# First attention of an eight-layer kernel: value products of two key tiles in a row, twice per unit

## The chip, the cores and the metric

One core of a Trainium2 chip runs the whole program. A core has five engines that are tied together by semaphores only: TensorE (matrix products, which read the working memory SBUF and write the accumulators, PSUM), VectorE, ScalarE, GpSimd and SyncE (which here issues the transfers, DMAs). The metric is the device time of one execution in microseconds (us). Smaller is better.

## What is computed

A residual stream `x` of 8 sequences x 512 tokens x 128 channels goes through four attention-like layers and four mixtures of experts. The change touches the first layer alone, an attention with 16 heads of 8 channels and a relative bias:

```python
xn = layernorm(layernorm(x)) * ln_g + ln_b
q, k, v = split_heads(xn @ w_qkv + b_qkv)          # 16 heads of 8
scores = einsum('bhqd,bhkd->bhqk', q, k) * scale
attn = softmax(scores + relative_bias(w_rel), axis=-1)
out = einsum('bhqk,bhkd->bhqd', attn, v)
x = x + merge_heads(out) @ w_out + b_out
```

## The kernel before

`relative_attention` (from line 839) is the stage. Its work is cut into 32 units: for each of the B = 8 sequences b, NG = 4 groups g of GH = 4 heads; unit u = 4 b + g. All engines walk through the units in an order that is written out by hand, each in its own function in the block, and wait for one another by semaphores.

For softmax the maximum over the keys is needed first. So the scores are made twice. `max_score(u, s)` (line 1099) makes a product of 128 queries by 512 keys in bf16 parts, 16 per unit, into one of three PSUM buffers `aps`; VectorE takes its maximum over the keys (`maximum`, line 1329). `turn_maxima` (line 1105) transposes the 16 columns of maxima into the next `aps` buffer, ScalarE copies them (`take_maxima`, line 1256), GpSimd splits them into three bf16 parts, and DMAs put those into rows of `Q`. Two units later `key_scores(u, t)` (line 1111) makes the product of 128 keys by 512 queries with the maximum already subtracted, 16 per unit, two per call, into one of three buffers `sps`, and ScalarE takes the exponential of it into `prob` (line 1293). Here A stands for a product of `max_score` and S for one of `key_scores`.

`values(u, k)` (line 1120) is the product of the probabilities with the values, in fp32: for key tile k (4 of them) four heads, each in its own 32 columns of TensorE, accumulated in the PSUM buffer `ops` over the four k. A fp32 product leaves two records in the trace, so that one call has 8. When all four k are done, ScalarE copies `ops` to `OT` (`copy_outputs`, line 1261). `turn_outputs` (line 1129) transposes it in four pieces into `mps`, and VectorE divides by the sum of the probabilities (`outputs`, lines 1337 and 1339).

Once per sequence there are further pieces of work on TensorE, in fp32, which share the one buffer `mps`: `turn_sequence` and `project` (lines 1136 and 1143) for the sequence before, in units g = 2 and g = 3; `v_part` (1161), `turn_tokens` (1150), `qk_part` (1155) for sequences to come, in units g = 0, g = 1 and g = 2, 3. `project` is followed by `add_output` on VectorE (1346) and by statistics (1350, 1354) in unit g = 3. ScalarE copies what the pieces made after the unit's exponentials, and `copy_sequence` after the fourth exponential of g = 2.

The order on TensorE in unit u: for t_ = 0 to 7 there is A(2 t_), S(2 t_), S(2 t_ + 1), A(2 t_ + 1), where the A belong to unit u + 2 and the S to unit u. After t_ = 0 comes the sequence or the projection, after t_ = 2 the output transposes of unit u - 2, after t_ = 6 the piece for a later sequence, and after t_ = 1, 3, 5, 7 the value products of unit u - 1 with k = 0, 1, 2, 3. At the end stands the turn of the maxima. An A waits until the maximum three buffers back is taken, an S until the exponential three back is done.

On VectorE the maxima s = 0 to 15 come in order, and `outputs(u - 2)` after s = 6. On SyncE each unit has the transfer of the maxima (`store_max`), in two of four units a store of the q or k parts that GpSimd has split (`store_parts`), and the nine loads of a unit three ahead (`load`). The first A of a unit waits for those loads.

Seven further stages follow, each in its own block.

Of the kernel before, what the change touches and what calls it, by code (L numbers as in the profile page):

```python
# [838 lines left out]
def relative_attention(nc, net, d):  # L839
# [16 lines left out]
    with ExitStack() as ctx:  # L856
# [223 lines left out]
        def _(pe):  # L1080
            def claim(*use):
                kind, n = before[use]
                emptied = dict(xt=xt_done, q=pj_done[0], k=pj_done[1], v=pj_done[2], outputs=o_done,
                               sequence=otn_done, project=y_added)[kind]
                pe.wait_ge(emptied, n + 1)

            def max_score(u, s):
                n = SLOTS * u + s
                if n >= 3:
                    v, r = (n - 3) // SLOTS, (n - 3) % SLOTS  # L1090
                    if r < NS:
                        pe.wait_ge(a_used, NS * v + r + 1)
                    else:
                        pe.wait_ge(mr_done, v + 1)
                if s == 0:
                    pe.wait_ge(qk_loaded[u % NG], LQ * (u // NG + 1))
                j, q = s // TC, s % TC
                head = GH * (u % NG) + j
                nc.tensor.matmul(aps[n % 3][:, :], Q[0:MAX, head, q * P:(q + 1) * P], K[0:MAX, head, :],  # L1099
                                 start=True, stop=True).then_inc(a_ready, 1)  # L1100

            def turn_maxima(u):
                n = SLOTS * u + NS
                pe.wait_ge(a_used, NS * (u + 1))
                nc.tensor.transpose(aps[n % 3][0:NS, 0:P], nm[u % 2][:, :], net.ident[:, :]).then_inc(a_ready, 1)

            def key_scores(u, t):
                for k in (2 * t, 2 * t + 1):
                    wait(pe, p_done, NS * u + k - 2)
                    head = GH * (u % NG) + k // TC  # L1110
                    nc.tensor.matmul(sps[(NS * u + k) % 3][:, :], K[0:KB, head, k % TC * P:(k % TC + 1) * P], Q[0:KB, head, :],  # L1111
                                     start=True, stop=True).then_inc(s_ready, 1)

            def values(u, k):
                if k == 0:
                    pe.wait_ge(p_done, NS * (u + 1))
                    pe.wait_ge(vg_ready, u + 1)
                    wait(pe, ot_copied, u)
                for j in range(GH):
                    last = nc.tensor.matmul(ops[32 * j:32 * j + 32, :], Vg[u % 2][:, k, j, :], prob[u % 2][:, j, k, :],  # L1120
                                            start=(k == 0), stop=(k == TC - 1))
                if k == TC - 1:
                    last.then_inc(av_done, 1)

            def turn_outputs(u):
                pe.wait_ge(ot_copied, u + 1)
                claim("outputs", u)
                for q in range(TC):
                    last = nc.tensor.transpose(mps[:, q * P:(q + 1) * P], OT[u % 2][:, q * P:(q + 1) * P], net.ident[:, :])
                last.then_inc(ott_done, 1)  # L1130

            def turn_sequence(b):
                pe.wait_ge(o_done, NG * (b + 1))
                claim("sequence", b)
                for q in range(TC):
                    last = nc.tensor.transpose(mps[:, q * P:(q + 1) * P], O[:, q, :], net.ident[:, :])
                last.then_inc(on_turned, 1)

            def project(b):
                pe.wait_ge(otn_done, b + 1)  # L1140
                claim("project", b)
                for q in range(TC):
                    last = nc.tensor.matmul(mps[:, q * P:(q + 1) * P], OTn[:, q * P:(q + 1) * P], wo[:, :],
                                            start=True, stop=True)
                last.then_inc(y_done, 1)

            def turn_tokens(c, to):
                pe.wait_ge(xn_done, c + 1)
                for k in range(TC):
                    last = nc.tensor.transpose(to[:, k * P:(k + 1) * P], xn[c % 2][:, k, :], net.ident[:, :])  # L1150
                last.then_inc(xt_ready, 1)

            def qk_part(n, c, to):
                pe.wait_ge(xt_done, c + 1)
                nc.tensor.matmul(to[:, :], w[:, n, :], net.xT[:, c * S:(c + 1) * S],
                                 start=True, stop=True).then_inc(pj_ready[n], 1)

            def v_part(c, to):
                pe.wait_ge(xt_done, c + 1)
                for k in range(TC):  # L1160
                    last = nc.tensor.matmul(to[:, k * P:(k + 1) * P], net.xT[:, c * S + k * P:c * S + (k + 1) * P],
                                            w[:, 2, :], start=True, stop=True)
                last.then_inc(pj_ready[2], 1)
# [26 lines left out]
            for b, g in units:  # L1190
                u = NG * b + g
                for t_ in range(8):
                    if u + 2 < U:
                        max_score(u + 2, 2 * t_)
                    if t_ == 0:
                        pe.wait_ge(max_loaded[u % 2], 48 * (u // 2 + 1))
                    key_scores(u, t_)
                    if u + 2 < U:
                        max_score(u + 2, 2 * t_ + 1)
                    if t_ == 0 and g == 2 and b >= 1:  # L1200
                        turn_sequence(b - 1)
                    if t_ == 0 and g == 3 and b >= 1:
                        project(b - 1)
                    if t_ == 2 and u >= 2:
                        turn_outputs(u - 2)
                    if t_ == 6:
                        if g == 0 and b + 1 < B:
                            claim("v", b + 1)
                            v_part(b + 1, mps)
                        if g == 1 and b + 2 < B:  # L1210
                            claim("xt", b + 2)
                            turn_tokens(b + 2, mps)
                        if g >= 2 and b + 2 < B:
                            claim("qk"[g - 2], b + 2)
                            qk_part(g - 2, b + 2, mps)
                    if t_ % 2 == 1 and u >= 1:
                        values(u - 1, t_ // 2)
                if u + 2 < U:
                    turn_maxima(u + 2)
# [90 lines left out]
        def _(v):  # L1310
# [15 lines left out]
            def maximum(u, s):  # L1326
                n = SLOTS * u + s
                v.wait_ge(a_ready, n + 1)
                nc.vector.tensor_reduce(nm[u % 2][:, s:s + 1], aps[n % 3][:, :], AX.X, ALU.max, negate=True).then_inc(a_used, 1)  # L1329

            def outputs(u):
                b, g = u // NG, u % NG
                v.wait_ge(ott_done, u + 1)
                if g == 0:
                    wait(v, on_turned, b)
                m = mps[:, :].rearrange("p (q j e) -> p q j e", q=TC, j=GH)
                nc.vector.reciprocal(den[:, :, :], m[:, :, :, HD]).then_inc(den_done, 1)
                v.wait_ge(den_done, u + 1)
                nc.vector.tensor_tensor(O[:, :, GH * HD * g:GH * HD * (g + 1)].rearrange("p q (j e) -> p q j e", e=HD),
                                        m[:, :, :, 0:HD], bcast(den[:, :, :], HD), ALU.mult).then_inc(o_done, 1)  # L1340

            def add_output(b):
                v.wait_ge(y_done, b + 1)
                v.wait_ge(bo_added, b + 1)
                xt = net.x[:, TC * b:TC * (b + 1), :].rearrange("p a b -> p (a b)")
                nc.vector.tensor_tensor(xt, xt, mps[:, :], ALU.add).then_inc(y_added, 1)
# [38 lines left out]
            for b, g in units:  # L1385
                u = NG * b + g
                for s in range(NS):
                    if u + 2 < U:
                        maximum(u + 2, s)
                    if s == 6 and u >= 2:  # L1390
                        outputs(u - 2)
                    if g == 3 and b >= 1:
                        if s == 1:
                            add_output(b - 1)
                        if 8 <= s < 8 + TC:
                            measure_tile(b - 1, s - 8)
                        if 12 <= s < 12 + TC:
                            settle_tile(b - 1, s - 12)
# [1592 lines left out]
```

## Time and profile before

| quantity | value |
| --- | --- |
| median of 3 runs | 2145.57 us (2142.47 to 2148.5) |
| the profiled execution | 2134.8 us |
| its span, first to last instruction | 2132.7 us |
| mean granted clock of TensorE | 0.798 |
| busy in the span: TensorE, VectorE, ScalarE, GpSimd | 1485.4, 1027.6, 742.3, 427.1 us |
| the first attention | from the start to about 500 us |

The profile is of one execution. Its timeline lists instructions with start and duration in us from the start of the span; instructions of one kind that follow each other are merged, with their count behind an x. PE is TensorE's product, PEld its load of weights, DVE VectorE, ACT ScalarE, POOL GpSimd, SPq the queue of SyncE. A bracket at the end gives the time for which the engine was idle just before, and which instruction ended that. Matmuls are pipelined: their records overlap, and what one of them costs is read from the distance between starts. A granted clock of 1.00 is 2.4 GHz, of 0.50 it is 1.2 GHz.

### The profile page before, as it was taken

The page shows a single profiled execution, that of the slowest core. Times are in us where ns is not written, and L with a number is a line of the kernel's source. Part 1 is how long each engine was busy: PE and PEld are TensorE (multiplying, and loading weights), DVE is VectorE, ACT ScalarE, POOL GpSimd, SP SyncE. Part 2 cuts the span into 40 slices and gives each one's busy share as a digit, 9 for nine tenths or more (in the row PEclk, how much of TensorE's full clock was granted, in tenths as well). Part 3 has the DMA queues.
Part 4 walks back from the last instruction along what each step waited for, and adds up shares of the span by engine and source line. Part 5 has one row for each costly group of instructions (what it writes and reads, how often), then busy time and mean ns, then how long its engine had stood idle before and what let it go on. Part 6 is the DMA issues. An engine that isn't in the chain of part 4 may idle for free. (4 is left out here: it accounts for less than half of the span.)

```text
span 2132.7 us, 24214 instructions
## 1 busy us (share of the span) xinstructions
PE 1485.4 (70%) x6978; PEld 807.4 (38%) x6979; DVE 1027.6 (48%) x2585; ACT 742.3 (35%) x1505; POOL 427.1 (20%) x604
## 2 busy tenths in 40 slices
PE   3899999996205870553369994776899436867767
PEld 1233333332103540232136661555366315754422
DVE  4888888874621223597612224445100346541445
ACT  1477777774001210562212222221423330014234
POOL 2433333310031004100034442000000012010036
PEclk6799999998557995586679995765899765558889
DMA  6111111100151111000074410000000000000001
GB/s 122 39 46 45 44 45 45 46 23 1 30 174 39 41 37 35 6 0 0 3 144 87 81 41 4 1 0 1 21 1 1 2 5 0 1 0 11 1 20 30
DMA packets 76061, 67.82 MB, mean 32 GB/s; under 512 B 17711, under 2 KB 63104, under 8 KB 75784
## 3 DMA queue, kind: packets, MB, share of 16 engines
q1 hardware_dynamic: 73911, 62.40, 12.0%
q0 software_dynamic: 2048, 4.20, 0.7%
q8 instruction: 48, 0.79, 0.1%
q14 instruction: 54, 0.43, 0.1%
HBM read 49.71 MB, written 16.41 MB: 31 GB/s over the span
## 5 line engine op out<-in xcount | busy, mean ns | idle before, releaser
L1329 DVE TENSOR_REDUCE a_nm<-a_aps 128x1 f32<-128x512 f32 x512 | 333.5, 687 | 90.7 <-PE a_aps L1099 90.7
L1293 ACT ACTIVATE a_prob<-a_sps 128x512 f32<-128x512 f32 x512 | 271.2, 597 | 112.5 <-PE a_sps L1111 111.6
L1099 PE MATMUL a_aps<-a_K,a_Q 96*128 96x512 bf16 x512 | 194.5, 400 | 23.8 <-DMA a_K<-k_parts 23.5
L1111 PE MATMUL a_sps<-a_Q,a_K 99*128 99x512 bf16 x512 | 155.5, 383 | 1.0 <-ACT a_prob L1293 1.0
L1120 PE MATMUL a_ops<-a_prob,a_Vg 128*32 128x512 f32 x1024 | 136.6, 608 | 0.0
L2018 POOL TENSOR_TENSOR m1e_h<-m1e_a,m1e_t 128x512 f32<-128x512 f32 x72 | 91.2, 1267 | 149.6 <-DVE m1e_t L2035 145.9
L2035 DVE TENSOR_TENSOR m1e_t<-m1e_G,m1e_gps 128x512 f32<-128x512 f32 x64 | 43.9, 688 | 136.8 <-PE m1e_gps L1964 109.9
L1099 PEld LDWEIGHTS a_aps<-a_K,a_Q 96*128 96x128 bf16 x512 | 50.0, 98 | 150.6 <-DVE a_nm L1329 89.6
L2006 ACT ACTIVATE m1e_a<-m1e_hps 128x512 f32<-128x512 f32 x72 | 43.0, 597 | 146.9 <-PE m1e_gps L1964 146.9
L2380 DVE TENSOR_TENSOR x_resid<-x_resid,m2e_yps 128x512 f32<-128x512 f32 x8 | 5.5, 688 | 159.2 <-PE m2e_yps L2330 159.2
L1964 PE MATMUL m1e_gps<-x_normT,m1e_w 128*128 128x512 f32 x144 | 75.8, 609 | 8.8 <-DVE m1e_t L2035 8.8
L1960 PE MATMUL m1e_hps<-x_normT,m1e_w 128*128 128x512 f32 x144 | 76.3, 612 | 8.1 <-DMA m1e_w<-in_L_ffn_ws 8.1
L1633 DVE TENSOR_TENSOR m0e_h<-m0e_hps,m0w_b 128x512 f32<-128x512 f32 x40 | 27.7, 692 | 111.4 <-PE m0e_hps L1587 111.4
L2371 ACT ACTIVATE m2e_h<-m2e_hps,m2e_b 128x512 f32<-128x512 f32 x64 | 43.1, 683 | 96.7 <-PE m2e_hps L2319 96.0
L1973 PEld LDWEIGHTS m1e_yps<-m1e_w,m1e_h 128*128 128x128 f32 x576 | 68.8, 192 | 13.8 <-issue 13.4
L1111 PEld LDWEIGHTS a_sps<-a_Q,a_K 99*128 99x128 bf16 x512 | 49.8, 98 | 61.2 <-ACT a_prob L1293 30.9
L115 PE MATMUL a_ln_tps<-ident,a_ln_xn 128*128 128x128 f32 x64 | 17.8, 435 | 77.3 <-DVE a_ln_xn L102 76.8
L1973 PE MATMUL m1e_yps<-m1e_w,m1e_h 128*128 128x128 f32 x576 | 69.1, 275 | 0.2 <-POOL m1e_h L2018 0.2
L1581 PE MATMUL m0e_xps<-ident,m0e_x 128*128 128x128 f32 x40 | 12.3, 309 | 77.8 <-DMA m0e_x<-rows_in 77.0
L2330 PE MATMUL m2e_yps<-m2e_W,m2e_h 128*128 128x128 f32 x512 | 65.6, 281 | 0.0
L2844 PE MATMUL m3e_yps<-m3e_WT,x_normT 128*128 128x512 f32 x128 | 61.4, 618 | 5.5 <-DVE x_resid L2894 5.5
L2319 PE MATMUL m2e_hps<-x_normT,m2e_W 128*128 128x512 f32 x128 | 62.2, 631 | 0.0
(470 smaller groups left out, 2867.8 us busy)
## 6 DMA issues: line engine op xcount, KB each, us to landing
m1e_G<-gates_by_expert SPq DMA_DIRECT2D x16, 1024.0 KB, 12.0
a_Q<-q_parts SPq DMA_DIRECT2D x192, 32.0 KB
q_parts<-a_partsq SPq DMA_DIRECT2D x8, 384.0 KB, 2.8
k_parts<-a_partsk SPq DMA_DIRECT2D x8, 384.0 KB, 2.8
a_K<-k_parts SPq DMA_DIRECT2D x32, 96.0 KB
rows_in<-m0w_zeros SPq DMA_DIRECT2D x1, 2560.0 KB, 11.0
m0e_x<-rows_in SPq DMA_DIRECT2D x40, 64.0 KB, 1.8
rows_out<-m0e_y SPq DMA_DIRECT2D x40, 64.0 KB, 1.6
```

The costliest lines, as they stand in the source:

```text
L1099: nc.tensor.matmul(aps[n % 3][:, :], Q[0:MAX, head, q * P:(q + 1) * P], K[0:MAX, head, :], start=True, stop=True).then_inc(a_ready, 1)
L1111: nc.tensor.matmul(sps[(NS * u + k) % 3][:, :], K[0:KB, head, k % TC * P:(k % TC + 1) * P], Q[0:KB, head, :], start=True, stop=True).then_ ...
L1120: last = nc.tensor.matmul(ops[32 * j:32 * j + 32, :], Vg[u % 2][:, k, j, :], prob[u % 2][:, j, k, :], start=(k == 0), stop=(k == TC - 1))
L1293: nc.scalar.activation(prob[u % 2][:, k // TC, k % TC, :], sps[n % 3][:, :], ACT.Exp).then_inc(p_done, 1)
L1329: nc.vector.tensor_reduce(nm[u % 2][:, s:s + 1], aps[n % 3][:, :], AX.X, ALU.max, negate=True).then_inc(a_used, 1)
L1960: nc.tensor.matmul(hps[u % 2][:, :], w1[:, j, :], net.xT[:, c * S:(c + 1) * S], start=True, stop=True)
L1964: nc.tensor.matmul(gps[u % 2][:, :], w3[:, j, :], net.xT[:, c * S:(c + 1) * S], start=True, stop=True).then_inc(up_done, 1)
L1973: last = nc.tensor.matmul(yps[c % 2][:, k, :], h[c % 2][:, j, k * P:(k + 1) * P], w2[:, j, :], start=(j == 0), stop=(j == NW - 1))
L2018: nc.gpsimd.tensor_tensor(h[c % 2][:, j, :], a[u % 3][:, :], t[u % 3][:, :], ALU.mult).then_inc(h_done, 1)
L2319: nc.tensor.matmul(hps[e % 4][:, :], W1[:, e, :], net.xT[:, c * S:(c + 1) * S], start=False, stop=True).then_inc(up_done, 1)
L2330: last = nc.tensor.matmul(yps[c % 2][:, k, :], h[c % 2][:, e, tok], W2[:, e, :], start=False, stop=(e == E - 1))
L2844: last = nc.tensor.matmul(yps[t % 3][:, HALF * q:HALF * (q + 1), :].rearrange("p e d -> p (e d)"), net.xT[:, t * P:(t + 1) * P], WT[:, HAL ...
```

## The change

On TensorE the value products for k = 0 and 1 now follow each other after t_ = 3, those for k = 2 and 3 after t_ = 7. The output transposes move from t_ = 2 to t_ = 3, directly ahead of the value products, and the piece for a later sequence moves from t_ = 6 to t_ = 7, directly ahead of the other pair. On VectorE `outputs(u - 2)` moves from behind the maximum s = 6 to behind s = 8. Nothing is added or taken away; sequence and projection stay after t_ = 0, and the value products of the last unit, which follow each other already, stay as they are.

```diff
@@ -1201,9 +1201,9 @@
                         turn_sequence(b - 1)
                     if t_ == 0 and g == 3 and b >= 1:
                         project(b - 1)
-                    if t_ == 2 and u >= 2:
+                    if t_ == 3 and u >= 2:
                         turn_outputs(u - 2)
-                    if t_ == 6:
+                    if t_ == 7:
                         if g == 0 and b + 1 < B:
                             claim("v", b + 1)
                             v_part(b + 1, mps)
@@ -1213,7 +1213,8 @@
                         if g >= 2 and b + 2 < B:
                             claim("qk"[g - 2], b + 2)
                             qk_part(g - 2, b + 2, mps)
-                    if t_ % 2 == 1 and u >= 1:
+                    if t_ % 4 == 3 and u >= 1:
+                        values(u - 1, t_ // 2 - 1)
                         values(u - 1, t_ // 2)
                 if u + 2 < U:
                     turn_maxima(u + 2)
@@ -1387,7 +1388,7 @@
                 for s in range(NS):
                     if u + 2 < U:
                         maximum(u + 2, s)
-                    if s == 6 and u >= 2:
+                    if s == 8 and u >= 2:
                         outputs(u - 2)
                     if g == 3 and b >= 1:
                         if s == 1:
```

## Rows read from the trace of the kernel before

**Rows 1.** Stretches: length, busy (x count) per engine, granted clock, DMA share, GB/s.

```profile
100.00:440.00 340.00, 330.05 (x1919) 120.18 (x1912) 282.07 (x503) 245.60 (x484) 127.24 (x240) 1.00 0.16 45
470.00:480.00 10.00, 9.24 (x61) 2.81 (x57) 0.69 (x3) 9.04 (x19) 2.12 (x6) 1.00 0.02 4
83.00:90.00 7.00, 6.12 (x24) 1.65 (x24) 3.88 (x6) 3.20 (x7) 1.14 (x3) 0.76 0.21 59
```

**Rows 2.** Timeline of TensorE within a unit: start, duration, engine, line, tiles, count.

```profile
208.62 0.60 PE L1129 MATMUL a_mps<-ident,a_OT 128*128 128x128 f32 x4
209.06 0.38 PE L1099 MATMUL a_aps<-a_K,a_Q 96*128 96x512 bf16 x1
209.28 0.60 PE L1111 MATMUL a_sps<-a_Q,a_K 99*128 99x512 bf16 x2
209.71 0.38 PE L1099 MATMUL a_aps<-a_K,a_Q 96*128 96x512 bf16 x1
210.02 1.07 PE L1120 MATMUL a_ops<-a_prob,a_Vg 128*32 128x512 f32 x8
211.02 0.39 PE L1099 MATMUL a_aps<-a_K,a_Q 96*128 96x512 bf16 x1
```

**Rows 3.** Timeline: turns of the maxima, SyncE's loads, and first A's behind them.

```profile
204.36 0.28 PE L1105 MATMUL a_aps<-ident,a_nm 128*16 128x128 f32 x1
...
217.55 0.28 PE L1105 MATMUL a_aps<-ident,a_nm 128*16 128x128 f32 x1
...
226.41 2.21 SPq L948 DMA_DIRECT2D a_Q<-q_parts  x6
...
231.20 0.28 PE L1105 MATMUL a_aps<-ident,a_nm 128*16 128x128 f32 x1
232.82 0.38 PE L1099 MATMUL a_aps<-a_K,a_Q 96*128 96x512 bf16 x1 [1.34 <-DMA a_K<-k_parts]
...
245.97 0.38 PE L1099 MATMUL a_aps<-a_K,a_Q 96*128 96x512 bf16 x1
```

**Rows 4.** Timeline of TensorE at the stage's end: four value groups in a row.

```profile
491.69 3.64 PE L1120 MATMUL a_ops<-a_prob,a_Vg 128*32 128x512 f32 x32
```

**Rows 5.** Timeline of VectorE where TensorE waits for it, and around outputs().

```profile
59.00 7.27 DVE L1329 TENSOR_REDUCE a_nm<-a_aps 128x1 f32<-128x512 f32 x12 [0.90 <-PE a_aps L1099]
59.75 0.10 PEld L1099 LDWEIGHTS a_aps<-a_K,a_Q 96*128 96x128 bf16 x1 [0.75 <-DVE a_nm L1329]
...
210.09 0.25 DVE L1337 RECIPROCAL a_den<-a_mps 128x16 f32<-128x16 f32 x1
210.37 0.29 DVE L1339 TENSOR_TENSOR a_O<-a_mps,a_den 128x128 f32<-128x128 f32 x1
210.57 0.68 DVE L1329 TENSOR_REDUCE a_nm<-a_aps 128x1 f32<-128x512 f32 x1
```

**Rows 6.** Timeline of ScalarE: maxima, first exponentials of a unit, exponentials back to back.

```profile
205.15 0.25 ACT L1256 ACTIVATE a_mr<-a_aps 16x128 f32<-16x128 f32 x1
205.31 2.20 ACT L1293 ACTIVATE a_prob<-a_sps 128x512 f32<-128x512 f32 x4
...
211.66 2.06 ACT L1293 ACTIVATE a_prob<-a_sps 128x512 f32<-128x512 f32 x4 [0.88 <-PE a_sps L1111]
```

**Rows 7.** Groups of instructions, 100 to 440 us: busy us, mean ns, idle before.

```profile
L1350 DVE BATCH_NORM_STATS2 a_bst<-x_resid 128x6 f32<-128x128 f32 x20 | 5.7, 283 | 0.0
L1354 DVE BATCH_NORM_AGGREGATE x_stat<-a_bst 128x2 f32<-128x6 f32 x20 | 3.4, 171 | 0.0
```

**Rows 8.** Timeline of TensorE: values and turn of a unit without a projection.

```profile
444.28 1.06 PE L1120 MATMUL a_ops<-a_prob,a_Vg 128*32 128x512 f32 x8
445.93 0.28 PE L1105 MATMUL a_aps<-ident,a_nm 128*16 128x128 f32 x1 [0.59 <-DVE a_nm L1329]
```

**Rows 9.** Timeline of TensorE: first S of unit 30 and first of unit 31.

```profile
470.31 0.60 PE L1111 MATMUL a_sps<-a_Q,a_K 99*128 99x512 bf16 x2
...
480.27 0.60 PE L1111 MATMUL a_sps<-a_Q,a_K 99*128 99x512 bf16 x2
```

**Rows 10.** Timeline of TensorE: a value group at the lower clock.

```profile
86.46 1.94 PE L1120 MATMUL a_ops<-a_prob,a_Vg 128*32 128x512 f32 x8
```

## What the change was predicted to do

> **What bounds the kernel now.** I read the table of stretches first, to see whether the stage is steady: between 100 and 440 us TensorE is busy 330 of 340 us at a granted clock of 1.00, VectorE 282, ScalarE 246 [rows 1]. Then TensorE's timeline, for the distance between starts: the durations overlap, so the distances are the prices. A score product (A, line 1099, or S, line 1111) takes a slot of 0.217 us: 209.28 and 209.71 are two slots apart. Four output transposes take 0.44 (208.62 to 209.06). Ahead of a group of value products the last A has 0.31 instead of 0.217 (209.71 to 210.02), and the next A starts 1.00 after the group (211.02) [rows 2]. One group costs 1.00 + 0.093 = 1.09 us. A unit is then 32 slots (6.93), four groups (4.37), transposes (0.44), a projection or the like (0.44 to 0.89, two in some units) and the turn of the maxima (0.11); the unit between the turns at 204.36 and 217.55 takes 13.19 [rows 3], and that is filled without a wait. The exceptions are the first A of units with g = 0 and g = 1, which wait for loads. After the turn that ends g = 2 (217.55) GpSimd splits the maxima and q, SyncE stores and loads (six of its nine loads at 226.41), and the first A of g = 0 starts at 232.82, 15.27 after the turn [rows 3]; six such chains measure 14.52 to 15.27, mean 14.9. From the turn that ends g = 3 (231.20) to the first A of g = 1 (245.97) it is 14.77, six of them 14.77 to 15.08, mean 14.9 again. A unit that ends inside its chain can't win anything, and growth is swallowed there first.
>
> **What the change removes.** Two groups in a row share one entry and one exit. The tail of the stage has four in a row: 3.64 us for 32 records, against 1.07 for one group's 8 [rows 2, 4]. Each added group costs (3.64 - 1.07) / 3 = 0.857 instead of 1.09. That is 0.234 a pair, two pairs a unit, 0.47 us in each of 31 units, 14.5 us of TensorE's time at most. Transposes and projections show no entry or exit of their own, so their new place beside the values is taken at nothing. If the entry of 0.093 hid behind them as well, a pair would give 0.33: my other end.
>
> The Trainium skill, TensorEngine Tiling (Array Packing), Key Properties, says that a change of tiling mode drains the engine; by that rule alone the time would fall by the 14.5, to 2131. The same page, under PSUM Bottleneck, warns that tiling speeds up the products and not the reading of PSUM, which may become the bottleneck; that speaks against this change, and the count of the readers follows.
>
> **What it adds.** A value group writes neither aps nor sps, so it is the pause in which VectorE and ScalarE catch up. Before, four or eight score slots were followed by 1.09 or 0.44 us of other work. Now sixteen slots come in one burst of 3.47 us, then 2.4 to 3.3 us of values and transposes. VectorE has eight maxima to take from a burst. Where it is the slow one they start (7.27 - 0.69) / 11 = 0.60 us apart. A reduction starts 0.41 after its A, and the A that takes its buffer again starts 0.06 after its end (reduction from 59.00, 0.69 long, A's weights at 59.75) [rows 5]: with three buffers, A(n+3) is no earlier than reduction(n) + 0.75. VectorE can't work ahead, and in the long pause it runs dry.
>
> Second half of a unit, from A8 at 0. Its reduction starts at 0.41. outputs() now stands behind it; the next reduction starts 0.61 + 0.28 + 0.20 later (reciprocal 210.09, product 210.37, reduction 210.57) [rows 5]. Reductions start at 0.41, 1.51, 2.11, 2.71, 3.31. A12 is due at 1.73 (slot 8) and needs 1.51 + 0.75 = 2.26: a wait of 0.53. A14 is then due at 3.13 and needs 2.71 + 0.75 = 3.46: 0.33. Sum 0.86. First half, from the turn: A0 at 0.11, A1 0.76, A2 0.98; reductions at 0.52, 1.17, 1.77, 2.37. A2 waits for ScalarE's copy of the maxima, which ends 1.04 after the turn (205.15 + 0.25 against 204.36) [rows 3, 6]; A6 needs 2.37 + 0.75 = 3.12 against 2.71 without any wait: 0.41 in all. A plain unit loses 1.27 and gains 0.47: +0.80 us.
>
> Unit g = 2 also copies the sequence on ScalarE behind the fourth exponential. Exponentials begin 0.95 after the turn and are (2.06 - 0.60) / 3 = 0.49 apart [rows 6]; S(n+3) is no earlier than exponential(n) + 0.66. With the copy's 0.60 the fifth starts at 3.62, so S7 needs 4.28; slot 14 and the 0.44 of the sequence transposes would put it at 3.58. First half 0.70, second 0.86: 1.56, net +1.09. In unit g = 3, add_output waits for project and holds VectorE from 2.07 to 2.67 after the turn, which costs the first half 0.42; in the second, four statistics and four aggregates (0.28 and 0.17 long, 0.20 and 0.08 in the queue) [rows 7] stand among the maxima, A12 to A15 need 2.46, 3.26, 4.06, 4.86 and the last is due at 3.25: 1.61. Together 2.03, net +1.56. Unit g = 0 loses 1.27 too, but the chain of loads that started at the turn ahead of it lasts 14.9; the unit comes to 13.54 and still ends inside. It costs nothing.
>
> **Sum.** A batch: 0.80 + 1.09 + 1.56 = 3.45 us; five of them (units 5 to 24) 17.2, less 0.4 since unit 5 has hardly a load wait ahead of it: 16.8. Units 1 and 2 add 1.0, unit 3's growth goes into the load wait behind it, unit 4 adds 0.8: 1.8. Units 25 to 29 have no projection, and TensorE waits there at the turn for the last maximum now (0.65 at 445.93) [rows 8]; that wait ends, the rest is as above: stepped through, +4.0. Units 30 and 31 have S alone, at ScalarE's pace: unit 30 ends 9.96 us after its start (480.27) [rows 9]; in bursts of eight S, each with S7 at the fifth exponential + 0.66, its halves come to 6.4 and 5.2 us: +1.7, unit 31 +1.1 for the same reason. Sum 16.8 + 1.8 + 4.0 + 2.8 = 25.4 us. The same steps with the order of before give 345.8 us for units 4 to 29; the trace has 347.2. The profiled execution took 2134.8 us for a span of 2132.7; with the change it would be 2160.2. The median of the runs lies 10.8 above that execution, a difference that the change doesn't touch: 2145.6 + 25.4 = 2171.
>
> **Bounds.** A pair that gives 0.33: 62 x 0.096, about 4.4 less after what the load chains keep. Reductions 0.65 apart in a burst, as where the A's themselves come 0.65 apart: 3.3 more. Rounding of a slot in the stepping, 0.1 us a unit: 3 either way. The case's own range: 2163 to 2178.
>
> **Rivals.** (1) The readers keep up, the other sign. If three buffers absorb the burst, units gain 0.47 and only the six of g = 0 keep nothing: 25 x 0.47 = 11.8 us, so 2134. It would take reductions about (3.47 + 0.4) / 8 = 0.48 us apart; against it stands the 0.60 [rows 5] and that TensorE waits for VectorE at the turn already [rows 8]. Chance 0.06. (2) Small loss: the pair gives 0.33 and the waits are half of those stepped through, because the first A's after a pause find all buffers free sooner than I count. The waits are 25.4 + 11.8 = 37.2 us; 18.6 less 25 x 0.66 = 16.5 leaves +2, 2148. Chance 0.06. (3) The clock falls. In 83 to 90 us, behind two long waits, the granted clock was 0.76 on average, that is 1.2 GHz for about half of it, and a value group took 1.94 instead of 1.07 [rows 1, 10]: 0.24 x 7 = 1.7 us lost. New waits in a burst close to the load wait of g = 1 could bring that once a batch: six times, +10, 2181. Against it: in 470 to 480 us, with a wait at every fourth S, the clock stayed at 1.00 [rows 1]. Chance 0.08. The Trainium skill, TensorE: Matmul & The Clock Gate, in its section on psum-queue depth-cycling, tells of a kernel whose short idles between groups made the clock go up and down; the row of 470 to 480 does not bear it out for idles of half a microsecond.
>
> **Chances.** Forecast 0.80, clock 0.08, small loss 0.06, readers keep up 0.06. Within 0.3% of now (2139 to 2152, about what a measurement of this kernel can tell from no change) lies the small loss: 0.05. Faster 0.05, slower 0.90. The range leaves out the two cheap cases and holds the forecast with its bounds and most of the clock case: 2159 to 2180.
>
> **What would show it.** In the profile after: waits of A for VectorE's reduction at A6 and at A12 to A14 of each unit, 0.3 to 0.5 us each; from turn to turn about 14.3, 14.2, 15.2 and 13.5 us for g = 1, 2, 3, 0 (with the load wait in that of the unit it precedes) instead of 13.2, 13.15, 13.6 and 14.2; a double value group with its next A 1.86 after its start. The load wait at g = 0 vanishes, that at g = 1 grows to about 1.3. All later stages keep their length. I am wrong if units of 12.7 us appear, if the waits are there but a pair gives far more than 0.23, or if value groups take 1.9 us each at half clock.

## The result, and the profile after

The changed kernel takes 2167.73 us in the median of four runs (2162.75 to 2172.76) against 2144.02 for the kernel before: a ratio of 1.0117, interval 1.0096 to 1.0137, or 23.7 us more (20.6 to 29.4 by the interval). Three executions of 3264 to 3805 us, two of the kernel before and one of e8 below, are left out of the ratios. The profiled execution took 2164.65 us with a span of 2162.7.

The same stretch as the first of [rows 1] and the two largest waits of TensorE in it, from the changed kernel (columns as in [rows 1]; in the waits: who waited for whom, us in total, times, longest):

```profile
100.00:440.00 340.00, 315.86 (x1812) 114.06 (x1811) 255.35 (x478) 234.13 (x461) 122.82 (x230) 1.00 0.16 44
```

```profile
PEld a_aps L1099 <- DVE a_nm L1330: 70.4, 157, 1.0
PEld a_sps L1111 <- ACT a_prob L1294: 27.7, 80, 0.8
```

TensorE is busy 316 us instead of 330 at the same clock. VectorE and ScalarE do less per microsecond as well (255 for 282, 234 for 246): nobody has become busier, and yet the stage is slower. That is the mark of engines that wait for each other in turn. The two waits above are those of the weight loads (PEld), which overlap the products, so that much of that time costs nothing: the kernel before has 66.3 us (84 times) and 17.4 us (52 times) in their place. What the products themselves stood idle for is in the groups of instructions of the same stretch, before and after:

```profile
L1099 PE MATMUL a_aps<-a_K,a_Q 96*128 96x512 bf16 x405 | 148.0, 381 | 9.7 <-DMA a_K<-k_parts 9.6
L1099 PE MATMUL a_aps<-a_K,a_Q 96*128 96x512 bf16 x384 | 137.2, 383 | 22.5 <-DVE a_nm L1330 15.5 <-DMA a_K<-k_parts 5.9
```

The idle time of A goes from 9.7 us, 9.6 of it for loads, to 22.5, of which 15.5 is for VectorE and 5.9 for loads. A unit with g = 2, timeline of TensorE in the changed kernel:

```profile
209.78 0.28 PE L1105 MATMUL a_aps<-ident,a_nm 128*16 128x128 f32 x1
...
213.25 0.38 PE L1111 MATMUL a_sps<-a_Q,a_K 99*128 99x512 bf16 x1
213.96 0.39 PE L1111 MATMUL a_sps<-a_Q,a_K 99*128 99x512 bf16 x1 [0.33 <-ACT a_prob L1294]
214.19 0.38 PE L1099 MATMUL a_aps<-a_K,a_Q 96*128 96x512 bf16 x1
214.41 0.60 PE L1129 MATMUL a_mps<-ident,a_OT 128*128 128x128 f32 x4
214.94 1.92 PE L1120 MATMUL a_ops<-a_prob,a_Vg 128*32 128x512 f32 x16
216.80 0.39 PE L1099 MATMUL a_aps<-a_K,a_Q 96*128 96x512 bf16 x1
...
218.32 0.38 PE L1099 MATMUL a_aps<-a_K,a_Q 96*128 96x512 bf16 x1
219.06 0.39 PE L1099 MATMUL a_aps<-a_K,a_Q 96*128 96x512 bf16 x1 [0.36 <-DVE a_nm L1330]
219.28 0.60 PE L1111 MATMUL a_sps<-a_Q,a_K 99*128 99x512 bf16 x2
219.72 0.38 PE L1099 MATMUL a_aps<-a_K,a_Q 96*128 96x512 bf16 x1
220.25 0.39 PE L1099 MATMUL a_aps<-a_K,a_Q 96*128 96x512 bf16 x1 [0.16 <-DVE a_nm L1330]
...
223.94 0.28 PE L1105 MATMUL a_aps<-ident,a_nm 128*16 128x128 f32 x1
```

The double group has its next A 1.86 after its start (214.94 to 216.80), 1.95 with its entry of 0.093, where two single ones as in [rows 2] take 2.18 with theirs. Against that stand the holes (S7 is the eighth S of the unit, and so on): S7 at 213.96, 0.71 after S6 instead of a slot of 0.22; A12 at 219.06, 0.74 after A11; A14 at 220.25, 0.53 after A13. Turn to turn it is 14.16 us, where [rows 3] have 13.19 for the same kind of unit. VectorE in that unit:

```profile
213.48 1.87 DVE L1330 TENSOR_REDUCE a_nm<-a_aps 128x1 f32<-128x512 f32 x3
217.22 0.69 DVE L1330 TENSOR_REDUCE a_nm<-a_aps 128x1 f32<-128x512 f32 x1 [1.87 <-PE a_aps L1099]
217.83 0.25 DVE L1338 RECIPROCAL a_den<-a_mps 128x16 f32<-128x16 f32 x1
218.11 0.29 DVE L1340 TENSOR_TENSOR a_O<-a_mps,a_den 128x128 f32<-128x128 f32 x1
218.32 4.27 DVE L1330 TENSOR_REDUCE a_nm<-a_aps 128x1 f32<-128x512 f32 x7
```

It takes the last three maxima of the first burst, stands idle for 1.87 us, takes one, does outputs(), and then runs seven in a row at (4.27 - 0.69) / 6 = 0.60 us with TensorE behind it. The readers idle in the pause and are late in the burst.

The loads, changed kernel, in the places of [rows 3]:

```profile
239.09 0.28 PE L1105 MATMUL a_aps<-ident,a_nm 128*16 128x128 f32 x1
239.20 0.38 PE L1099 MATMUL a_aps<-a_K,a_Q 96*128 96x512 bf16 x1
...
252.65 0.28 PE L1105 MATMUL a_aps<-ident,a_nm 128*16 128x128 f32 x1
254.16 0.38 PE L1099 MATMUL a_aps<-a_K,a_Q 96*128 96x512 bf16 x1 [1.23 <-DMA a_K<-k_parts]
```

The wait ahead of g = 0 is gone, that ahead of g = 1 is 1.51 from the turn.

All runs are compared in one table. Work is the time from a unit's first A to its turn of the maxima, the load wait what lies between the turn before and that A, the turn's own 0.11 included (both means over units 8 to 23, g = 0, 1, 2, 3 and g = 0, 1); units 0 to 29 run from the turn ahead of unit 0 to that of unit 29; the tail from there to the last statistic of the stage. The times of a row come from one profile, the ratio to the kernel before from all runs but the three named above.

| kernel | work of a unit | load waits | units 0 to 29 | tail | ratio (interval) |
| --- | --- | --- | --- | --- | --- |
| before | 12.72, 12.27, 13.08, 13.54 | 1.40, 0.76 | 401.5 | 31.9 | |
| changed | 13.46, 13.00, 14.04, 15.03 | 0.11, 1.29 | 421.6 | 35.5 | 1.0117 (1.0096 to 1.0137) |
| e12, changed again | 13.46, 13.00, 14.05, 15.04 | 0.11, 1.25 | 423.5 | 35.5 | 1.0124 (1.0099 to 1.0149) |
| e1, outputs() behind s = 7 | 13.02, 12.57, 13.61, 14.55 | 0.28, 1.56 | 412.7 | 35.3 | 1.0040 (1.0015 to 1.0064) |
| e2, moves only | 12.72, 12.26, 13.08, 14.00 | 0.82, 1.28 | 403.8 | 33.4 | 1.0003 (0.9980 to 1.0026) |
| e3, pairs only | 12.45, 12.00, 13.35, 13.46 | 1.31, 0.98 | 401.3 | 34.5 | 1.0013 (0.9994 to 1.0032) |
| e6, pairs and outputs | 13.13, 12.68, 13.72, 14.33 | 0.41, 1.40 | 414.5 | 35.5 | 1.0084 (1.0057 to 1.0111) |
| e7, pairs and piece | 12.77, 12.31, 13.66, 14.17 | 0.59, 1.39 | 407.5 | 34.0 | 1.0043 (1.0021 to 1.0065) |
| e5, before, half maxima | 12.72, 12.27, 13.08, 13.54 | 1.33, 1.03 | 401.2 | 32.0 | 0.9950 (0.9931 to 0.9969) |
| e4, changed, half maxima | 12.67, 12.22, 13.41, 13.52 | 1.48, 0.65 | 401.4 | 35.5 | 0.9963 (0.9936 to 0.9990) |
| e9, before, both halved | 12.67, 12.21, 13.08, 13.54 | 1.45, 0.83 | 401.2 | 30.6 | 0.9941 (0.9922 to 0.9960) |
| e10, changed, both halved | 12.17, 11.72, 12.59, 13.41 | 1.52, 1.04 | 389.6 | 31.0 | 0.9896 (0.9862 to 0.9930) |
| e8, one pair | 12.87, 12.03, 12.84, 13.29 | 1.72, 0.87 | 400.1 | 32.0 | 0.9978 (0.9963 to 0.9994) |
| e11, one pair again | 13.25, 12.03, 12.84, 13.29 | 1.90, 0.72 | 401.0 | 32.0 | 1.0004 (0.9987 to 1.0021) |

Beyond units 0 and 1, where every kernel has TensorE at the lower clock for a time, units 0 to 29 of e3, e4, e5 and e9 hold one spell of low clock each, at unit 4, worth some 1.5 us (below); e8 holds two and e11 three. The kernels with halved maxima also save 7 us ahead of unit 0, where VectorE paces the first sixteen products.

### The profile page after: what moved, and what is told of

It is laid out like the page before. It is cut to its first block and busy times, and to the rows that moved or that the text cites. A ratio compares the mean times of both kernels' runs of the same rounds, so it can differ in the third digit from the quotient of the medians.

```text
span 2162.7 us, 24214 instructions
## 1 busy us (share of the span) xinstructions
PE 1493.4 (69%) x6978; PEld 813.4 (38%) x6979; DVE 1014.0 (47%) x2585; ACT 742.8 (34%) x1505; POOL 427.4 (20%) x604
## 5 line engine op out<-in xcount | busy, mean ns | idle before, releaser
L1330 DVE TENSOR_REDUCE a_nm<-a_aps 128x1 f32<-128x512 f32 x512 | 319.7, 681 | 124.6 <-PE a_aps L1099 124.6
L1120 PE MATMUL a_ops<-a_prob,a_Vg 128*32 128x512 f32 x1024 | 122.9, 598 | 0.0
L1634 DVE TENSOR_TENSOR m0e_h<-m0e_hps,m0w_b 128x512 f32<-128x512 f32 x40 | 27.7, 692 | 111.6 <-PE m0e_hps L1588 111.6
```

## The experiments

Theory A is that of the prediction: without the value groups between them the score products come in bursts that two readers with three buffers each can't follow, and the pauses are lost to the readers. Rivals: B, the pairs or the fp32 work next to them cost TensorE time by themselves; C, the later place of transposes and projection is what costs.

e1 to e12 are the kernels of the table.

**The parts one by one.** The moves alone, on the kernel before:

```diff
-                    if t_ == 2 and u >= 2:
+                    if t_ == 3 and u >= 2:
...
-                    if t_ == 6:
+                    if t_ == 7:
...
-                    if s == 6 and u >= 2:
+                    if s == 8 and u >= 2:
```

> The kernel before with the moves alone: output transposes after t_ = 3, the piece after t_ = 7, outputs() behind s = 8; value products one at a time after t_ = 1, 3, 5, 7 as before. Theory A: value groups still break the bursts, so only unit g = 3 waits (A14 0.37 us); stepped through, 3 us more than before, about 2147 us. Theory C (the later place of the transposes and the projection is what costs, through the buffer mps and ScalarE's copies at the end of the unit): most of the 24 us is there already, about 2165 us.

The ratio is 1.0003; units g = 3 grew from 13.54 to 14.00, the others not at all, and the load wait ahead of g = 0 took most of that. The median is 2141.6 where 2147 was expected: the 5 us by which the stage ends later in the profile (507.2 for 502.1) are not seen in the runs, though their interval just holds them. C, which asked for 2165, is out.

The pairs alone:

```diff
-                    if t_ % 2 == 1 and u >= 1:
+                    if t_ % 4 == 3 and u >= 1:
+                        values(u - 1, t_ // 2 - 1)
                         values(u - 1, t_ // 2)
```

> The kernel before with the pairing alone: value products of two key tiles after t_ = 3 and t_ = 7, everything else where it was (transposes after t_ = 2, piece after t_ = 6, outputs() behind s = 6). Theory A: the transposes and the piece break each burst after twelve of its sixteen products, so that nearly no wait is left (0.1 to 0.4 us a unit) and the 0.47 us of the pairs is won where no load chain takes it: 2 to 3 us less than before, 2142 us. Theory B: the pairs themselves cost; 2160 us or more. A reading in which the pair alone makes the burst would give half or more of the 24 us.

Ratio 1.0013, median 2146.2 for the 2142 expected. Units g = 0 and g = 1 are 0.27 shorter, so a pair costs nothing by itself: B is out in its plain form. But the 2 to 3 us that I expected to win did not come. The tail, where ScalarE paces, grew by 2.6 us, which I had not counted. Unit 4 took 14.01 us of work instead of 12.45 in a spell of low clock, on which more below. And unit g = 2 grew from 13.08 to 13.35. TensorE and ScalarE of e3 in that unit:

```profile
208.42 0.38 PE L1099 MATMUL a_aps<-a_K,a_Q 96*128 96x512 bf16 x1
209.25 0.63 PE L1129 MATMUL a_mps<-ident,a_OT 128*128 128x128 f32 x4 [0.46 <-ACT a_OTn L1267]
```

```profile
207.53 1.08 ACT L1294 ACTIVATE a_prob<-a_sps 128x512 f32<-128x512 f32 x2 [0.16 <-PE a_sps L1111]
208.50 0.61 ACT L1267 ACTIVATE a_OTn<-a_mps 128x512 f32<-128x512 f32 x1
```

The output transposes need the buffer mps, which copy_sequence holds until 209.11. With a value group at t_ = 1 that copy was hidden; without it TensorE meets it. That unit g = 3 is only 0.08 shorter (13.54 to 13.46) was not followed up.

Pairs with one of the two moves each:

```diff
 e6: pairs, and
-                    if t_ == 2 and u >= 2:
+                    if t_ == 3 and u >= 2:
-                    if s == 6 and u >= 2:
+                    if s == 8 and u >= 2:
 e7: pairs, and
-                    if t_ == 6:
+                    if t_ == 7:
```

> The kernel before with the pairs and with the output transposes after t_ = 3 and outputs() behind s = 8; the piece stays after t_ = 6. Theory A: the first burst is whole again (0.4 us of waits at A6, 0.6 at S7 in g = 2) and outputs() delays the second (0.5 at A12); units 14.0, 13.9, 14.4 and 13.6 us for g = 1, 2, 3, 0; some 15 to 17 us more than before, about 2160 us. If instead the losses of the two parts simply add (pairs alone 3.6 us, moves alone 5.2 us at the stage's end), under 2152 us.

> The kernel before with the pairs and with the piece after t_ = 7; output transposes and outputs() stay after t_ = 2 and s = 6. Theory A: only the end of the second burst lacks its break (0.3 us at A14); stepped through 5 us more than before from the second to the last turn, with the tail's 2.6 and the wait of the transposes for ScalarE's copy of the sequence in g = 2 some 9: about 2152 us.

The medians are 2160.9 and 2152.1, as stepped through. Units 0 to 29 and tail, against before: pairs alone +2.4 us, moves alone +3.8, pairs and outputs +16.7, pairs and piece +8.1, everything +23.7. The two halves of the change cost 6 us if taken one at a time and 24 together. Either the value groups or the transposes and the piece are enough to break a burst; when both leave, sixteen score products stand in a row. A good part of the interaction is the place of outputs(): behind s = 8 it is part of the 3.8 us with single groups, and with pairs it costs 8.9 us by itself (e1, next). This is the strongest evidence for A, since no fixed cost of any single operation can behave like that.

**The place of outputs().** The changed kernel, with VectorE's part one maximum earlier:

```diff
-                    if s == 8 and u >= 2:
+                    if s == 7 and u >= 2:
```

> The changed kernel, with outputs() on VectorE behind the maximum s = 7 instead of s = 8; TensorE's order is that of the change. Theory A (bursts of sixteen score products run VectorE dry and then wait for it): outputs() now runs in the pause that the two value groups make, so the wait of A12 falls from 0.53 to about 0.08 us while that of A14 stays at 0.3; units from turn to turn 14.2, 13.8, 14.65 and 13.2 us for g = 1, 2, 3, 0; stage about 10 us shorter than with the change, so about 2158 us. Theory B (the paired value groups, or fp32 work next to them, cost TensorE time by themselves): no difference to the change, 2168 us.

Measured 14.13, 13.72, 14.66 and 13.30 from turn to turn, the expected numbers to within 0.1, and 8.9 us less in units 0 to 29. It would be 10, as expected, but for units 0 and 1, which took 1.3 us more between them with a spell of low clock there twice as long. The median is 2151.56, ratio 1.0040, better than the 2158 expected; the span of the profile is 8.2 below that of the changed kernel (2154.5 for 2162.7), and where the rest of the median's gain comes from is not shown. More than a third of the change's loss is one reciprocal and one product on VectorE that stood behind A8, whose reduction can't start before the pause is over, when it could have run in the pause.

**The readers made faster.** Half of the keys in VectorE's maxima, on both kernels:

```diff
-                nc.vector.tensor_reduce(nm[u % 2][:, s:s + 1], aps[n % 3][:, :], AX.X, ...
+                nc.vector.tensor_reduce(nm[u % 2][:, s:s + 1], aps[n % 3][:, 0:256], AX.X, ...
```

> The changed kernel with each of VectorE's maxima in the first attention taken over 256 of the 512 keys; the other half is left out of the maximum, all else is the same. Theory A: a reduction then takes some 0.42 us instead of 0.69, VectorE keeps up with a burst and A's waits for it go; units 13.1, 13.6, 13.6, 13.9 us; the change's loss falls from 24 to about 1 us: 2145 us. What is left are ScalarE's waits in g = 2. Theory B: the loss stays, 2165 us.

> The kernel before with each of VectorE's maxima in the first attention taken over 256 of the 512 keys (the other half is left out); the partner of the changed kernel with the same shortening. Theory A: before, no unit waited for VectorE except at the turn of units without a piece, so from the second to the last turn only 1 to 2 us go (401.5 to about 400); the two units at the start of the stage, which VectorE paces, lose 7 us as they did in the partner. About 2136 us, equal to the partner's 2138 within noise: with fast reductions the change's order costs nothing. Theory B: the partner is 20 us slower than this one.

Units 0 to 29 take 401.4 and 401.2 us: the loss of 20.1 us has gone to 0.2. In the tail, which ScalarE paces, the loss stays (35.5 for 32.0). The medians are 2138.0 and 2132.0 (2145 and 2136 expected), with ratios whose intervals overlap. And in units 0 to 29 the changed order isn't faster either, though its value groups save 0.47 a unit. Waits in the stretch 100 to 440 us of e4:

```profile
PEld a_sps L1111 <- ACT a_prob L1294: 58.7, 182, 0.9
```

The next reader has moved up: exponentials 0.49 apart against a slot pair of 0.433, and the weight loads of S wait 58.7 us for it where the changed kernel has 27.7. So the exponentials were shortened too, on top of the halved maxima. Both kernels then leave half of the queries out of the exponentials from unit 2 on, the other half of `prob` keeps older values, and their output is not that of the reference:

```diff
+                    w = 512 if u < 2 else 256
-                    nc.scalar.activation(prob[u % 2][:, k // TC, k % TC, :], sps[n % 3][:, :], ACT.Exp).then_inc(p_done, 1)
+                    nc.scalar.activation(prob[u % 2][:, k // TC, k % TC, 0:w], sps[n % 3][:, 0:w], ACT.Exp).then_inc(p_done, 1)
```

> The kernel before with both readers of the first attention shortened: VectorE's maxima over 256 of 512 keys, and from unit 2 on ScalarE's exponentials over 256 of 512 queries (the other halves keep older values). Theory A: before, TensorE alone paces the units and the load chains the first A's, so units stay 12.7, 12.3, 13.1 and 13.5 us of work for g = 0 to 3; first maxima 7 us faster as in its neighbours, tail of the stage 5 us shorter since ScalarE paced it: about 2128 us.

> The changed kernel with both readers shortened in the same way as its partner. With VectorE alone shortened the trace showed waits for ScalarE of 0.42 us a unit (0.1 at S5, S7, S13, S15, 0.58 at S7 in g = 2), which ate the gain of the pairs. Theory A: these go too, and the gain of the pairs stands alone: 12.25, 11.8, 12.6 and 13.1 us of work for g = 0 to 3, 0.47 less than the partner's; the load chains keep that of the units g = 3, so from the second to the last turn 11 us less than the partner, about 2117 us. Theory B (pairs save nothing in the flow, the 0.857 of the tail was a special case): same as the partner.

The mean durations in e10 (groups of instructions, 100 to 440 us: busy us, mean ns, idle before):

```profile
L1331 DVE TENSOR_REDUCE a_nm<-a_aps 128x1 f32<-128x256 f32 x417 | 162.2, 418 | 156.2 <-PE a_aps L1099 144.7
L1295 ACT ACTIVATE a_prob<-a_sps 128x256 f32<-128x256 f32 x417 | 137.5, 382 | 120.2 <-PE a_sps L1111 117.9
```

The wait of S for ScalarE is down from 58.7 us to 3.9. Now the change is a gain: 389.6 against 401.2 us for units 0 to 29, 11.5 less (11 expected), or 10 without the spell of low clock that e9 has and e10 hasn't, with 0.49 or 0.50 off the work of units g = 0, 1 and 2 and 0.13 off that of g = 3, where 0.47 was expected too. The medians are 2118.8 and 2128.0 (2117 and 2128 expected). The pair's 0.234 us is real in the flow; before, the readers were too slow to let it be seen.

**An order that keeps the bursts short.** On the kernel before, one pair a unit, single groups at t_ = 1 and 4, the piece at t_ = 5:

```diff
-                    if t_ == 6:
+                    if t_ == 5:
...
-                    if t_ % 2 == 1 and u >= 1:
-                        values(u - 1, t_ // 2)
+                    if u >= 1:
+                        one_by_one, one_pair = {1: (0,), 3: (1,), 5: (2,), 7: (3,)}, {1: (0,), 4: (1,), 7: (2, 3)}
+                        for k in (one_pair if u + 2 < U else one_by_one).get(t_, ()):
+                            values(u - 1, k)
```

> A new order: value products k = 0 after t_ = 1, k = 1 after t_ = 4, k = 2 and 3 as a pair after t_ = 7; the piece after t_ = 5; transposes and outputs() where they were before; units 30 and 31 as before. Theory A: no burst is longer than twelve score products without a break and the long pause comes once a unit, so that no wait is left and 0.234 us is won in units that no load chain holds: units 12.9, 12.9, 13.35 us for g = 1, 2, 3; stage 5 us shorter than before, 2139 us. Theory B (a pair costs by itself): slower than before.

> The order with one pair a unit once more, for a second profile and a narrower interval. In its first profile the units were 0.24 us shorter as expected, but two load chains took 16.6 us instead of 14.9 and ate most of that. If that was scatter of the transfers, the chains are 14.5 to 15.3 here, units 0 to 29 take 397 us and the median stays 4 to 5 us below the kernel before (ratio 0.998). If the order itself delays the transfers, chains of 16 us and more come back and the stage is no shorter than before.

The units are as expected, 0.24 shorter for g = 1, 2 and 3, and no product in them waits. The stage is not: 400.1 and 401.0 us, ratios 0.9978 and 1.0004, together no proven gain. Of the two readings in the second expectation neither is right as it stands. The chains of 16.4 to 16.7 us that end ahead of units 5 and 9 are long because the unit that they span, 4 or 8, is: TensorE's clock falls there. Its timeline in e8 behind the turn of unit 3, and the stretch around it:

```profile
124.17 0.28 PE L1105 MATMUL a_aps<-ident,a_nm 128*16 128x128 f32 x1
126.66 0.38 PE L1099 MATMUL a_aps<-a_K,a_Q 96*128 96x512 bf16 x1 [2.21 <-DMA a_K<-k_parts]
...
127.98 1.06 PE L1111 MATMUL a_sps<-a_Q,a_K 99*128 99x512 bf16 x2
128.83 0.63 PE L1099 MATMUL a_aps<-a_K,a_Q 96*128 96x512 bf16 x1
129.40 1.78 PE L1120 MATMUL a_ops<-a_prob,a_Vg 128*32 128x512 f32 x8
```

```profile
124.00:132.00 8.00, 5.79 (x26) 1.67 (x23) 3.14 (x5) 3.16 (x7) 5.79 (x11) 0.79 0.14 21
```

The S are 0.43 apart instead of 0.217, and the value group takes 1.78, of 1.07 at full clock and 1.94 in [rows 10]. The shorter unit g = 3 ends earlier, its load chain does not, and the wait ahead of g = 0 grows. In e8 and e11 it was 2.48, 2.46, 2.24, 2.50 and 1.82 us ahead of five units g = 0, and these took 14.0 to 14.06 us of work; the others from unit 4 to 24, behind 1.2 to 1.7 us, took 12.48. So each of the five gave back 1.5 us, while before, with at most 1.69 ahead of units 4 to 24, none did. In part the transfers are late as well. The six loads of Q start 8.8 us after the turn everywhere, but the stretch in which they are issued, at most 2.8 us long in each of the other twelve profiles, is longer in e8 and e11 at the same two units, 8 (3.02 and 3.71) and 21 (3.49 and 3.42): the order of e8 has a part in it. SyncE's queue ahead of unit 8 in e11:

```profile
173.27 3.71 SPq L948 DMA_DIRECT2D a_Q<-q_parts  x6
```

The chains into unit 8 took 15.87 and 15.90 us and those into unit 21 15.54 and 15.92, against at most 15.27 before; those into units 4 and 12 took 14.81 to 15.22, as before. What stretches the issue there stays open, and so does why unit 4 waits longer in some kernels than in others.

**The changed kernel once more.**

> The changed kernel once more, for a second profile. The first attention should end 24 us later than before again (526 us), with units of 14.1, 14.15, 15.15 and 13.6 us. The decay attention much further on took 156.4 us in the first profile against 153.4 before; if that is scatter from execution to execution, it may be any of the values seen so far (150 to 162 us), and the median stays 1.01 of before.

The units repeat to 0.01 us. The stage ended at 529.5 instead of 526.3: the turn ahead of unit 0 came 1.2 us later, and unit 1 and its load wait took 18.3 us for 16.1, in a spell of low clock near the start that was twice as long. The decay attention took 150.4 us this time, against 156.4; the median, 2163.47, is 1.0124 of before.

## Why the prediction was right

It said 2171 us; 2168 came. By its own steps, in the profiled execution:

- **Pair.** 1.86 to the next A and 0.53 from the transposes to the group (214.41 to 214.94), that is 0.44 and the entry of 0.093: the first as taken from the tail [rows 4], the second as in [rows 2]. The other end, an entry that hides behind fp32 work, is refuted for the transposes.
- **Second half of a unit.** Waits at A12 and A14 of 0.52 and 0.31 (0.53 and 0.33 predicted).
- **Units.** Work grew by 0.74, 0.73, 0.96 and 1.49 for g = 0, 1, 2, 3; predicted were 0.80, 0.80, 1.09 and 1.56. The small excess is in the first half: in g = 2, S7 waits 0.49 and A6 0.08, 0.57 where I had 0.70.
- **g = 0 costs nothing.** Its load wait fell from 1.40 to 0.11, and that ahead of g = 1 rose from 0.76 to 1.29, as the fixed chain demands.
- **Sum.** Units 1 to 4: 1.7 (predicted 1.8), but by luck in its parts: units 1 and 2, for which 1.0 was counted, added 0.55, all of it in unit 2 (unit 1 has 13.40 and 13.38 us of work), and unit 3's growth of 0.7 went only in part into the load wait behind it (1.69 to 1.37). Units 5 to 24: 15.0 (16.8); the excess above, 0.07, 0.13 and 0.07 for g = 1, 2 and 3 in each of five batches, is 1.35 of the 1.8, and the rest lies in the load waits at both ends. Units 25 to 29: 3.4 (4.0). Tail: 3.6 (2.8). The start gives 0.5 that no step had. The stage ends 24.3 us later, at 526.3 for 502.1.
- **Outside the stage.** The span grew by 30.0, not 24.3. I had said that the later stages keep their length; in this pair of profiles the decay attention, much further on, adds 3.0 us and the rest of the later stages 2.7. The decay attention took 156.4 us in the profile after and 153.4 in that of before, and in the other profiles 150.1 to 162.4, whatever was changed in the first stage. That is scatter which a single pair of profiles puts down to the change. The medians are 23.7 apart, 20.6 to 29.4 by the interval, so that they agree with 24.3 and could not tell it from the 25.4 forecast.
- **Rivals.** Readers that keep up: not with reductions of 0.69, but near enough in e10, where the 11.8 us of that rival were 11.5, or 10 without the spell of low clock in the partner. Clock: not in the changed kernel, where the load wait ahead of g = 0 vanished; it struck in e8 and e11 instead, and at unit 4 of e3, e4, e5 and e9, by another way than I had described, behind a wait for loads and not through bursts. Small loss: no.
- **What I missed.** That the output transposes wait for copy_sequence once the value group between them is gone (e3). In the changed kernel it doesn't show, since the transposes moved too. The tail's growth, 3.6 for 2.8, is of the same kind: TensorE and ScalarE waiting in turn.

The two-part structure was not foreseen: I had priced the move of the transposes at nothing beside outputs(), and the prediction charges the whole loss to the burst that the pairs leave. e2 and e3 show that neither is to blame alone.

## What to carry to other kernels

Work on an engine that doesn't feed the others' buffers is a pause for them; before it is bunched to save its entry and exit (here 0.234 us a pair), step through the burst that is left between, with the readers' spacing and the number of buffers. Put side work of a reader where it runs dry, not behind the first product of the next burst: one line in e1 gave back 8.9 us. And a gain ahead of a fixed chain of loads turns into a longer wait, behind which the clock may fall, and that can cost more than was gained.

## What the runs showed of the hardware

TensorE's clock did not fall in 340 us of bursts with three to five waits of 0.1 to 0.7 us in each unit (granted clock 1.00 in the changed kernel), but it did behind single waits for loads. Over all fourteen profiles, units 4 and later had thirteen such waits of 1.82 to 2.58 us from turn to first A. Behind nine of them (1.82 to 2.50 us) the products came at half rate for a while, at a cost of some 1.5 us each; behind four (1.83, 1.87, 2.25 and 2.58) they did not, nor behind any of 1.81 us or less. The longest of all cost nothing, so the length of the wait alone does not settle it. By the Trainium skill, TensorE: Matmul & The Clock Gate, in its section on psum-queue depth-cycling, short idles between groups made the clock go up and down in another kernel; for idles of this size no run here shows it.

The products of the decay attention come at the lower clock for most of its length, and the stage's length goes from 150.1 to 162.4 us in steps of 3 between executions. Stretches of that stage in e3 and e7:

```profile
1760.00:1911.00 151.00, 114.26 (x544) 89.91 (x544) 93.69 (x136) 4.93 (x8) 26.42 (x9) 0.58 0.00 1
```

```profile
1762.00:1925.00 163.00, 126.61 (x544) 101.62 (x544) 93.85 (x136) 4.93 (x8) 26.46 (x9) 0.53 0.00 0
```

The same 544 products and the same work on VectorE, 12 us apart, with a granted clock of 0.58 and 0.53. Most of what the medians of this kernel scatter by would fit in there; that it is the cause was not tested.
